# Graph kernel: tile 1's sources load first, and tile 0's counts are made after tile 1's attention

## The chip, the core and the metric

The kernel runs on one core of a Trainium2 chip. The metric is the device time of one execution in microseconds (us); three runs of the kernel before are given, and one further execution was profiled. The engines are PE (TensorE), DVE (VectorE), ACT (ScalarE), POOL (GpSimd) and SP (SyncE, which here only issues DMAs).

## The reference

A graph has 6,250 nodes with 128 features and 200,000 edges sorted by destination. An attention layer runs over the edges, then a layer norm, then two relational layers, then a layer norm:

```python
e = leaky_relu((h[src] @ Ws.T + h[dst] @ Wd.T + emb_rel[etype] @ Wr.T) @ attn_fc2_w.T, 0.01)
alpha = segment_softmax(e, dst)
agg = segment_sum(alpha[:, None] * h[src], dst)      # h itself where a node has no edge
x = layernorm(x + agg + h @ loop_weight)
for W_r, W_sl, W_el in two relational layers:
    self_msg = where(no_edge[:, None], h @ W_el, h @ W_sl)
    msg = (rel_embed[etype] + h[src]) @ W_r
    h = rrelu(segment_sum(msg, dst) * deg_isqrt + self_msg)
x = layernorm(x + h)
```

## The kernel before

**Tiles.** The nodes are cut into 50 tiles (`NT`) of 125 destinations. The edges of a tile lie in a window of 4,224 list entries, held as 128 partitions by 33 columns. A first stage loops over the tiles t = 0 to 49: it computes the attention and the first layer norm of tile t, and builds `counts[t]`, which says how many edges run from each source node to each destination of the tile. A second stage, the two relational layers, is one long row of matmuls with these counts, read back from memory, and starts when the first stage is done.

**One tile of the first stage.** SP loads the tile's lists: sources (`srcw`), destinations (`dstw`), types (`etw`), the node rows (`xt`), and in `load_wide` the destinations and types once more, broadcast to all partitions (two DMAs of 1,056 KB). POOL gathers the 4,224 source rows with 33 indirect DMAs into `rows[q]`, q = t % 2 (L559); it may start when the tile's lists are there and when PE has read what tile t - 2 left in that half (`acc_c`). DVE compares the lists with the tile's node numbers (`prepare_wide` and `prepare_edges`, one-hot masks); PE turns them into the edge terms of the attention (`terms`); ACT copies these out, SP writes them to memory and reads them back in another shape (`reshape_terms`), and DVE adds them up (DVE's `terms`). `weights` is the softmax over the edges: DVE computes `u`, and `z` at its end, with two exchanges with PE between. ACT then scales the 33 masks by exp(z), and PE multiplies them with the gathered rows (L875). DVE finishes the tile with `finalize` and `normalise`.

**Counts.** `records` packs the edge lists on DVE into 32-edge records, which SP stores. POOL gathers them (L552, 10 indirect DMAs) once for all tiles, DVE unpacks them (`recc`), PE turns them (L890) and ACT copies them to `idx`. From `idx` DVE makes one-hots in seven batches a tile, PE multiplies them (L805) and ACT copies the products into `AT`. SP's `store_counts(t)` writes `AT` to memory, 1,562.5 KB.

**What sets the order.** Each engine runs its instructions in the order in which its function is written and waits on semaphores. PE, ACT and DVE share two PSUM slots in turn, by the table `SEQ`. SP is one such order too:

```python
for t in range(NT):
    if t + 2 < NT:
        f2 = load_lists(t + 2)
        load_wide(t + 2, f2)
    ...
    if t + 1 < NT:
        reshape_terms(t + 1)
    ...
    if t < NT - 1:
        store_x1(t)
    store_counts(t)
```

So the lists of tile t + 2 are issued behind `store_counts(t - 1)`, which waits for ACT's last copy of tile t - 1's counts.

## Time and profile before

| what | value |
|---|---|
| median of 3 runs (lowest, highest) | 2778.87 us (2776.01 to 2779.62) |
| the profiled execution: its time, its span | 2776.1 us, 2774.0 us |
| mean granted TensorE clock | 0.906 |
| busy: PE, DVE, POOL, ACT | 2149.1, 2045.1, 1591.4, 1223.8 us |

Times in the rows are counted from the start of the span; the execution's own time is 2.1 us more than its span. The busy times say little alone, since the two stages have different limits: POOL works only in the first one, and PE's long row of matmuls fills the second.

### The profile page before, as it was taken

The numbers are of one execution on the slowest core, as the hardware profiler recorded it, in microseconds if no ns is written. First come the engines' busy times: TensorE is split into PE (matmuls) and PEld (weight loads), VectorE is DVE, ScalarE is ACT, GpSimd is POOL, SyncE is SP. The second block draws the span as 40 slices with busy tenths as digits, with TensorE's granted clock in tenths as the row PEclk, the third lists the DMA queues.
The fourth block names the chain that finished last, engine by engine and source line by source line (L and its number), as shares of the span: only waits on it lengthen the run. The fifth ranks groups of instructions, "written<-read, shape, count | busy, mean of one in ns | idle before, by whom it ended". The sixth has DMA issues, their size and how long they took to land.

```text
span 2774.0 us, 45483 instructions
## 1 busy us (share of the span) xinstructions
PE 2149.1 (77%) x16208; PEld 1802.6 (65%) x16208; DVE 2045.1 (74%) x4582; ACT 1223.8 (44%) x3215; POOL 1591.4 (57%) x1672
## 2 busy tenths in 40 slices
PE   1366676667767777777787788788787999999998
PEld 0255565556666666666676676676675876888887
DVE  5889998887888888888888888888797456333333
ACT  1255665555556456555555555555555323000000
POOL 6767777777777777777777777777774000000000
PEclk9988887888888988888889888999899999999999
DMA  8545554554555554554555555555454354666664
GB/s 219 145 126 173 173 153 153 157 165 152 160 175 151 156 181 146 159 183 148 160 186 151 160 190 153 168 183 156 148 177 152 112 156 133 215 211 211 217 211 158
DMA packets 184632, 463.50 MB, mean 167 GB/s; under 512 B 86336, under 2 KB 113784, under 8 KB 164577
## 3 DMA queue, kind: packets, MB, share of 16 engines
q1 hardware_dynamic: 116050, 339.10, 36.4%
q0 software_dynamic: 53600, 114.17, 16.4%
q10 hardware_dynamic: 14752, 7.26, 1.0%
q8 instruction: 132, 2.16, 0.3%
q14 instruction: 98, 0.80, 0.1%
HBM read 362.54 MB, written 97.84 MB: 166 GB/s over the span
## 4 chain that ended last, share of the span: by engine, by line
POOL 50%; PE 25%; issue 17%; DVE 6%; DMA 1%; ACT 1%; SPq 1%; ACTq 0%; POOLq 0%; DVEq 0%
POOL arena L559 50%; PE pair L951 19%; DVE arena L1114 2%; PE bank L875 1%; PE pair L924 1%; PE bank L836 1%; PE pair L954 1%; DMA wlp<-n_L_gnn_loop_weight_dram 1%; DVE arena L1084 1%; PE pair L805 1%; PE pair L782 0%; DMA group_starts<-endv 0%; SPq L434 0%; DVE arena L1194 0%; DVE arena L1092 0%
## 5 line engine op out<-in xcount | busy, mean ns | idle before, releaser
L559 POOL DMA_INDIRECT arena<-rows,srcw x1617 | 1541.6, 953 | 518.8 <-issue 491.4
L1114 DVE TENSOR_TENSOR arena<-bank,idx 128x2000 bf16<-128x2000 bf16 (+3 forms) x700 | 560.4, 853 | 21.1 <-PE pair L805 17.9
L951 PE MATMUL pair<-arena 125*125 125x384 bf16 x3285 | 551.4, 326 | 1.6 <-DVE arena L1316 1.6
L805 PE MATMUL pair<-arena 128*128 128x250 bf16 x2500 | 348.9, 287 | 260.0 <-DVE arena L1114 206.5
L581 ACT ACTIVATE arena<-pair 99x264 f32<-99x264 f32 (+2 forms) x410 | 279.0, 712 | 593.8 <-PE pair L805 448.5
L951 PEld LDWEIGHTS pair<-arena 125*125 125x125 bf16 x3285 | 447.4, 136 | 103.3 <-issue 8.4
L675 ACT ACTIVATE arena<-arena,wexp 128x128 f32<-128x128 bf16 x1650 | 487.4, 387 | 1.6
L875 PE MATMUL bank<-arena 128*125 128x130 f32 x3300 | 485.2, 318 | 0.0
L875 PEld LDWEIGHTS bank<-arena 128*125 128x125 f32 x3300 | 474.6, 230 | 4.2
L805 PEld LDWEIGHTS pair<-arena 128*128 128x128 bf16 x2500 | 239.7, 102 | 339.4 <-DVE arena L1114 267.0
L1084 DVE TENSOR_TENSOR arena<-arena,bank 128x4224 bf16<-128x4224 int16 x150 | 344.2, 2350 | 1.7
L1314 DVE SCALAR_TENSOR_TENSOR arena<-pair,norm,arena 125x128 f32<-125x128 f32 x99 | 34.6, 350 | 315.3 <-PE pair L954 270.9
L836 PE MATMUL bank<-arena 125*125 125x384 bf16 x1275 | 217.8, 328 | 2.1 <-DVE arena L1203 2.1
L782 PE MATMUL pair<-arena 128*125 128x200 bf16 x1650 | 191.4, 287 | 19.6 <-DVE arena L1114 19.6
L782 PEld LDWEIGHTS pair<-arena 128*125 128x125 bf16 x1650 | 189.5, 167 | 22.2 <-issue 20.3
L836 PEld LDWEIGHTS bank<-arena 125*125 125x125 bf16 x1275 | 170.1, 136 | 44.6 <-issue 13.9
L722 ACT ACTIVATE rstd<-mv,epst 125x1 f32<-125x1 f32 x50 | 14.7, 294 | 406.5 <-DVEq L1356 406.5
L1114 DVE TENSOR_TENSOR arena<-bank,et 128x6600 bf16<-128x6600 bf16 x50 | 179.2, 3584 | 0.0
L616 ACT ACTIVATE arena<-pair 128x500 bf16<-128x500 f32 x150 | 95.8, 638 | 72.7 <-PE pair L805 72.0
L1146 DVE TENSOR_TENSOR u<-arena,dr 128x33 f32<-128x33 f32 x50 | 10.8, 216 | 151.7 <-DMA arena<-rows,srcw 151.4
L1114 DVE TENSOR_TENSOR arena<-bank,dl 128x4224 bf16<-128x4224 bf16 x50 | 117.9, 2357 | 1.7
L795 PE MATMUL bank<-onesb,arena 128*125 128x1 bf16 x50 | 11.5, 230 | 131.2 <-issue 128.6
(250 smaller groups left out, 2312.6 us busy)
## 6 DMA issues: line engine op xcount, KB each, us to landing
arena<-counts SPq DMA_DIRECT2D x106, 812.5 KB, 4.4
counts<-arena SPq DMA_DIRECT2D x50, 1562.5 KB
arena<-dst SPq DMA_DIRECT2D x50, 1056.0 KB
arena<-etype SPq DMA_DIRECT2D x50, 1056.0 KB
arena<-rows,srcw POOLq DMA_INDIRECT x1617
arena<-counts SPq DMA_DIRECT2D x14, 281.2 KB, 2.8
edge_terms<-arena SPq DMA_DIRECT2D x200, 12.4 KB
xt<-in_x_dram SPq DMA_DIRECT2D x50, 62.5 KB
```

Source lines behind the costliest of these rows:

```text
L559: pool.indirect_dma_start(out=rows[:, q, c, :], out_offset=None, in_=rows0, in_offset=bass.IndirectOffsetOnAxis(ap=srcw[:, q, c:c + 1], ax ...
L581: act.activation(o, i, ACT.Copy).then_inc(s("ev"), 1)
L616: act.activation(AT[:, :, d0:d0 + 2 * G], two, ACT.Copy)
L675: r = act.activation(hot[:, c, :], hotb[:, c, :], ACT.Copy, scale=wexp[:, c:c + 1])
L782: r = pe.matmul(b_[0:TN, 0:R], hotb[:, c, 0:TN], toh[:, c, :], start=(c == 0), stop=(c == C - 1))
L805: r = pe.matmul(group_of(n, gi), ohl[:, sl, gi * GC + c, :], ohm[:, sl, gi * GC + c, :], start=(c == 0), stop=(c == GC - 1))
L836: pe.matmul(o, AT[0:TN, h, :], hs0[0:TN, h, :], start=(h == 0), stop=False)
L875: r = pe.matmul(sums[0:TN, 0:D + 2], hot[:, c, 0:TN], rows[:, q, c, 0:D + 2], start=(c == 0), stop=(c == C - 1))
L951: r = pe.matmul(o, ring[0:TN, m % RD, h - h0, :], hs[k][0:TN, h, :], start=(h == first), stop=(h == last - 1))
L1084: return v.tensor_tensor(out_.rearrange("p (j t) -> p j t", t=2), list_.rearrange("p (j t) -> p j t", t=2), two[:, None, :].broadcast_to(s ...
L1114: return v.tensor_tensor(hot_.rearrange("p c (j t) -> p c j t", t=2), iotap[:, 0:w].rearrange("p (j t) -> p j t", t=2)[:, None, :, :].broa ...
L1314: link(v.scalar_tensor_tensor(o, b_[0:TN, 0:D], n_, acc[0:TN, t, :], ALU.mult, ALU.add))
```

## The change

Seven things move, and nothing is computed otherwise.

1. The sources of a tile get a semaphore of their own (`ld_s0`, `ld_s1`), and POOL waits for them alone instead of for all three lists.
2. At the start of the fast path SP issues the sources of tile 1 first, then the broadcast lists of tile 0, then the short lists and node rows of tiles 0 and 1. Before, it was the padding record, the short lists of tile 0, its broadcast lists, and the lists of tile 1.
3. On POOL the wait for the lists of tile 2 stands behind the gather of the records.
4. On DVE `first_scores` comes first of all.
5. On DVE `records` comes behind the one-hots of tile 0.
6. On DVE, PE and ACT the turning of the records and the seven count batches of tile 0 go from loop turn 0 to turn 1, behind the attention weights of tile 1; `SEQ` is changed to match.
7. `normalise(0)` and the first layer's node step of tile 0 stand in front of them.

```diff
@@ order of the PSUM slots (SEQ)
     if t_ == 0:
         SEQ["types", 1] = len(SEQ)
         SEQ["turned", 1] = len(SEQ)
+        continue
+    if t_ == 1:
         for b_ in range(NGB):
             SEQ["idx", b_] = len(SEQ)
+        for j_ in range(BT):
+            SEQ["cnt", 0, j_] = len(SEQ)
     for j_ in range(BT):
         SEQ["cnt", t_, j_] = len(SEQ)
...
@@ sp_fast
-            def load_lists(t):
-                first = sp.value_load(plan_i[0:1, t:t + 1], min_val=0, max_val=E - WIN)
+            def load_sources(t, first):
+                sp.dma_start(srcw[:, t % 2, :], src[bass.ds(first, WIN)].rearrange("(p c) -> p c", c=C)).then_inc(s("ld_s%d" % (t % 2)), 16)
+
+            def window(t):
+                return sp.value_load(plan_i[0:1, t:t + 1], min_val=0, max_val=E - WIN)
+
+            def load_lists(t, first):
                 if t >= 2:
                     sp.wait_ge(s("u_done"), t - 1)
-                for a, w in ((src, srcw), (dst, dstw), (etype, etw)):
-                    if t >= 1 or a is not src:
-                        sp.dma_start(w[:, t % 2, :], a[bass.ds(first, WIN)].rearrange("(p c) -> p c", c=C)).then_inc(s("ld_w%d" % (t % 2)), 16)
+                if t >= 2:
+                    load_sources(t, first)
+                for a, w in ((dst, dstw), (etype, etw)):
+                    sp.dma_start(w[:, t % 2, :], a[bass.ds(first, WIN)].rearrange("(p c) -> p c", c=C)).then_inc(s("ld_w%d" % (t % 2)), 16)
...
+            f1 = window(1)
+            load_sources(1, f1)
+            f0 = window(0)
+            sp.wait_ge(s("st_l16"), 64)
+            load_wide(0, f0)
+            load_lists(0, f0)
+            load_lists(1, f1)
             sp.wait_ge(s("pad_ready"), 1)
             sp.dma_start(rec[E // GRAN:E // GRAN + 6], agg2[0:6, 0, 0:2 * GRAN]).then_inc(s("st_rec"), 16)
-            f0 = load_lists(0)
-            sp.wait_ge(s("st_l16"), 64)
-            load_wide(0, f0)
-            f1 = load_lists(1)
             load_wide(1, f1)
             reshape_terms(0)
...
@@ pool_fast
             for t in range(1, NT):
                 q = t % 2
-                pool.wait_ge(s("ld_w%d" % q), 48 * (t // 2 + 1) - (0 if q else 16))
                 if t == 2:
...
+                pool.wait_ge(s("ld_s%d" % q), 16 * (t // 2 + q))
                 if t >= 2:
                     pool.wait_ge(s("acc_c"), NAC * (t - 1))
...
@@ pe_fast (act_fast moves its copies in the same way)
-                if 1 <= t < NT - 1:
-                    row(t - 1)
-                if t == 0:
-                    types_in(1)
-                    types(1)
+                if t == 1:
                     for b in range(NGB):
                         n = seq("idx", b)
...
                     for j in range(BT):
                         batch(0, j)
+                if 1 <= t < NT - 1:
+                    row(t - 1)
+                if t == 0:
+                    types_in(1)
+                    types(1)
                     x1_in(0)
                     x1_node(0)
...
@@ dve_fast
+            first_scores()
             for k in range(2):
                 v.wait_ge(s("relW_ps"), k + 1)
...
-            records()
             v.wait_ge(s("st_rows"), ROWS_STORED)
             prepare_wide(0)
-            first_scores()
             prepare_edges(0)
+            records()
             terms(0)
...
                 if t == 0:
                     finalize(0)
                     prepare_edges(1)
+                    normalise(0)
+                if t == 1:
                     for b in range(NGB):
                         v.wait_ge(s("ld_rec%d" % b), 16)
...
                     for j in range(BT):
                         batch(0, j)
-                    normalise(0)
-                elif more:
+                if t >= 1 and more:
                     for j in range(2):
                         batch(t, j)
```

SP at the start of the fast path, before (`arena<-dst` and `arena<-etype` are the two broadcast lists, `edge_records<-agg` the padding record):

```order
L495 DMA edge_records<-agg 6x64 [waits pad_ready]
L441 TENSOR_LOAD plan_i
L441 ISA x2
L446 REGISTER_ALU
L446 DMA dstw<-in_dst_dram 128x33
L446 DMA etw<-in_edge_type_dram 128x33
L447 DMA xt<-in_x_dram 125x128
L454 REGISTER_ALU [waits st_l16]
L454 DMA arena<-dst 128x4224
L454 DMA arena<-etype 128x4224
```

and in the changed kernel:

```order
L448 TENSOR_LOAD plan_i
L448 ISA x2
L445 REGISTER_ALU
L445 DMA srcw<-in_src_dram 128x33
L448 TENSOR_LOAD plan_i
L448 ISA x2
L463 REGISTER_ALU [waits st_l16]
L463 DMA arena<-dst 128x4224
L463 DMA arena<-etype 128x4224
L456 REGISTER_ALU
L456 DMA dstw<-in_dst_dram 128x33
L456 DMA etw<-in_edge_type_dram 128x33
```

The sources of tile 1 go from the seventh DMA to the first, and tile 0's node rows (`xt`) from in front of the two broadcast lists to behind them.

SP in loop turn 0 of the changed kernel, from the read-back of tile 1's edge terms on (`dense_input` is `store_x1(0)`, `counts` is `store_counts(0)`, and the last two rows are the first lists of turn 1, those of tile 3):

```order
L473 DMA drw<-edge_terms 128x3x33 [waits dr_summed,dr_stored]
L485 DMA dense_input<-arena 125x128 [waits x1_ready]
L479 DMA counts<-arena 128x6250 [waits wm,ev]
L481 DMA counts<-arena 128x250 [waits ev]
L445 REGISTER_ALU [waits u_done]
L445 DMA srcw<-in_src_dram 128x33
L456 DMA dstw<-in_dst_dram 128x33
```

This piece reads as before: the sources of tile 3 still come behind the store of tile 0's counts, and that store still waits for ACT's copies (`ev`), which now belong to turn 1.

DVE at the end of turn 0 and the start of turn 1, before (the last count batches of tile 0, `normalise(0)`, the edge terms and `u` of tile 1):

```order
L1114 TENSOR_TENSOR arena<-bank,idx 128x1500 [waits pb]
L1114 TENSOR_TENSOR arena<-bank,idx 128x768
L1185 RECIPROCAL norm<-nv 125x1 [waits rs1]
L1186 RECIPROCAL nv<-nv 125x1
L1187 TENSOR_SCALAR arena<-arena,mv,nv 125x128 [waits dve_seq]
L1136 TENSOR_TENSOR dr<-drw 128x33 [waits ld_dr]
L1137 TENSOR_TENSOR dr<-dr,drw 128x33 [waits dve_seq]
L1146 TENSOR_TENSOR u<-arena,dr 128x33 [waits gath1,dr_summed]
```

and in the changed kernel, behind the one-hots of tile 1:

```order
L1148 TENSOR_SCALAR LS<-dstB 128x33
L1201 RECIPROCAL norm<-nv 125x1 [waits rs1,dve_seq]
L1202 RECIPROCAL nv<-nv 125x1
L1203 TENSOR_SCALAR arena<-arena,mv,nv 125x128 [waits dve_seq]
L1152 TENSOR_TENSOR dr<-drw 128x33 [waits ld_dr]
L1153 TENSOR_TENSOR dr<-dr,drw 128x33 [waits dve_seq]
L1162 TENSOR_TENSOR u<-arena,dr 128x33 [waits gath1,dr_summed]
```

`u` of tile 1 now follows the one-hots of its tile directly, with nothing of the counts in between.

## Rows read from the trace of the kernel before

**Rows 1.** The page, part 4: the chain that ended last, by line.

```profile
POOL arena L559 50%; PE pair L951 19%; DVE arena L1114 2%; PE bank L875 1%; PE pair L924 1%; PE bank L836 1%; PE pair L954 1%; DMA wlp<-n_L_gnn_loop_weight_dram 1%; DVE arena L1084 1%; PE pair L805 1%; PE pair L782 0%; DMA group_starts<-endv 0%; SPq L434 0%; DVE arena L1194 0%; DVE arena L1092 0%
```

**Rows 2.** Timeline of POOL: start us, us, instruction [idle before, releaser].

```profile
50.60 0.94 POOL L539 DMA_INDIRECT arena<-in_x_dram,srcw  x1 [0.30 <-issue]
...
67.43 0.95 POOL L559 DMA_INDIRECT arena<-rows,srcw  x1 [15.89 <-DMA etw<-in_edge_type_dram]
...
183.65 0.94 POOL L559 DMA_INDIRECT arena<-rows,srcw  x1 [10.82 <-PE bank L875]
```

**Rows 3.** Who waited for whom, whole run: us in total, times, longest us.

```profile
POOL arena L559 <- PE bank L875: 11.4, 3, 10.8
```

**Rows 4.** Timeline of PE, four places.

```profile
59.58 0.47 PE L753 MATMUL bank<-ident,xt 125*128 125x125 f32 x1 [13.33 <-DMA xt<-in_x_dram]
...
144.85 1.39 PE L890 MATMUL pair<-ident,arena 128*128 128x128 f32 x8
...
182.82 0.30 PE L772 MATMUL pair<-arena,Zd 125*3 125x264 bf16 x4
...
220.81 0.30 PE L772 MATMUL pair<-arena,Zd 125*3 125x264 bf16 x4
```

**Rows 5.** Timeline of DVE, from the first relation product to tile 2's preparation.

```profile
62.10 0.29 DVE L1063 CAST relW<-pair 128x128 bf16<-128x128 f32 x1 [18.46 <-PE pair L847]
...
93.43 3.48 DVE L1091 TENSOR_TENSOR arena<-arena 128x3200 f32<-128x3200 f32 x1
...
102.98 0.28 DVE L1121 TENSOR_SCALAR dl<-dstw,thr 128x66 bf16<-128x66 int32 x1
...
110.27 0.21 DVE L1146 TENSOR_TENSOR u<-arena,dr 128x33 f32<-128x33 f32 x1
...
115.51 0.41 DVE L1154 TENSOR_TENSOR_SCAN XY<-full,bank 1x128 f32<-1x128 f32 x1 [4.42 <-PE bank L862]
...
118.55 0.28 DVE L1099 TENSOR_TENSOR arena<-xt,bank 125x128 f32<-125x128 f32 x1
...
130.72 0.16 DVE L1170 TENSOR_SCALAR iso<-bank 125x1 f32<-125x1 f32 x1 [3.02 <-PE bank L875]
...
152.55 0.42 DVE L1227 COPY idx<-arena 128x100 bf16<-128x100 bf16 x2 [1.38 <-ACT arena L581]
...
171.70 0.29 DVE L1099 TENSOR_TENSOR arena<-xt,bank 125x128 f32<-125x128 f32 x1
```

**Rows 6.** Timeline of SP's DMA issues: start us, us, destination<-source.

```profile
59.87 0.52 SPq L446 DMA_DIRECT2D etw<-in_edge_type_dram  x1
...
132.81 0.34 SPq L454 DMA_DIRECT2D arena<-dst  x1
...
143.56 0.39 SPq L464 DMA_DIRECT2D drw<-edge_terms  x1
...
173.14 0.34 SPq L470 DMA_DIRECT2D counts<-arena  x1
...
175.47 0.34 SPq L446 DMA_DIRECT2D srcw<-in_src_dram  x1
```

**Rows 7.** Windows: us; length; PE, PEld, DVE, ACT, POOL busy; PEclk, DMA share, GB/s.

```profile
50.00:58.00 8.00, 0.00 (x0) 0.00 (x0) 0.00 (x0) 0.00 (x0) 1.24 (x2) 1.00 0.77 244
58.00:66.00 8.00, 2.97 (x11) 2.29 (x11) 3.49 (x13) 0.28 (x1) 0.00 (x0) 1.00 0.82 291
...
174.00:179.00 5.00, 5.00 (x32) 5.00 (x32) 5.00 (x3) 5.00 (x18) 0.00 (x0) 0.66 0.89 339
179.00:182.00 3.00, 3.00 (x30) 3.00 (x29) 2.97 (x4) 2.82 (x10) 0.00 (x0) 1.00 0.09 26
```

**Rows 8.** The DMA view: issues, count, KB each, median us to landing.

```profile
srcw<-in_src_dram SPq DMA_DIRECT2D x50, 16.5 KB, 2.1
...
arena<-in_x_dram,srcw POOLq DMA_INDIRECT x33, 9.4
```

**Rows 9.** Timeline of ACT: the last copy of tile 0's counts.

```profile
165.94 0.44 ACT L617 ACTIVATE arena<-pair 128x250 bf16<-128x250 f32 x1
```

More of the change, by code:

```diff
@@ L439, in sp_fast @@
         def sp_fast(sp):
-            def load_lists(t):
-                first = sp.value_load(plan_i[0:1, t:t + 1], min_val=0, max_val=E - WIN)
+            def load_sources(t, first):
[3 more added lines that the diff above has]
+            def load_lists(t, first):
                 if t >= 2:
                     sp.wait_ge(s("u_done"), t - 1)
-                for a, w in ((src, srcw), (dst, dstw), (etype, etw)):
-                    if t >= 1 or a is not src:
-                        sp.dma_start(w[:, t % 2, :], a[bass.ds(first, WIN)].rearrange("(p c) -> p c", c=C)).then_inc(s("ld_w%d" % (t % 2)), 16)
+                if t >= 2:
+                    load_sources(t, first)
+                for a, w in ((dst, dstw), (etype, etw)):
+                    sp.dma_start(w[:, t % 2, :], a[bass.ds(first, WIN)].rearrange("(p c) -> p c", c=C)).then_inc(s("ld_w%d" % (t % 2)), 16)
                 sp.dma_start(xt[0:TN, t % 3, :], x[t * TN:(t + 1) * TN]).then_inc(s("ld_xt%d" % (t % 3)), 16)
-                return first
             def load_wide(t, first):
@@ L506, in sp_fast @@
                 if t + 2 < NT:
-                    f2 = load_lists(t + 2)
+                    f2 = window(t + 2)
+                    load_lists(t + 2, f2)
                     load_wide(t + 2, f2)
@@ L686, in act_fast @@
                     types(1)
-                    for b in range(NGB):
-                        n = seq("idx", b)
-                        act_evac(act, n, idx[:, b * GB:(b + 1) * GB, :], slot(n)[:, :].rearrange("p (m g) -> p g m", g=GB))
-                    for j in range(BT):
-                        batch(0, j)
                     node_t(0)
@@ L694, in act_fast @@
                 elif t < NT - 1:
+                    if t == 1:
+                        for b in range(NGB):
+                            n = seq("idx", b)
+                            act_evac(act, n, idx[:, b * GB:(b + 1) * GB, :], slot(n)[:, :].rearrange("p (m g) -> p g m", g=GB))
+                        for j in range(BT):
+                            batch(0, j)
                     for j in range(3):
@@ L1057, in dve_fast, with first_scores @@
         def dve_fast(v, link):
+            def first_scores():
+                v.wait_ge(s("gath_x"), 16 * C)
+                for c0, c1 in ((0, XP), (XP, C)):
+                    w = c1 - c0
+                    link(v.tensor_tensor(prod[:, 0:w, :], rows[:, 0, c0:c1, 0:D], vb[:, None, 0:D].broadcast_to([P, w, D]), ALU.mult))
+                    link(v.tensor_reduce(rows[:, 0, c0:c1, D], prod[:, 0:w, :], AX, ALU.add))
+            first_scores()
             for k in range(2):
@@ L1085, in matches @@
                                        two[:, None, :].broadcast_to(shape), ALU.is_equal)
-            def first_scores():
-                v.wait_ge(s("gath_x"), 16 * C)
-                for c0, c1 in ((0, XP), (XP, C)):
-                    w = c1 - c0
-                    link(v.tensor_tensor(prod[:, 0:w, :], rows[:, 0, c0:c1, 0:D], vb[:, None, 0:D].broadcast_to([P, w, D]), ALU.mult))
-                    link(v.tensor_reduce(rows[:, 0, c0:c1, D], prod[:, 0:w, :], AX, ALU.add))
             def prepare_wide(t):
@@ L1119, in prepare_edges @@
                 q = t % 2
-                v.wait_ge(s("ld_w%d" % q), 48 * (t // 2 + 1) - (0 if q else 16))
+                v.wait_ge(s("ld_w%d" % q), 32 * (t // 2 + 1))
                 v.tensor_scalar(dl2[:], dstw[:, q, :][:, :, None].broadcast_to([P, C, 2]), thr[:, t:t + 1], None, ALU.subtract)
@@ L1277, in dve_fast @@
                     prepare_edges(1)
+                    normalise(0)
+                if t == 1:
                     for b in range(NGB):
@@ L1302, in dve_fast @@
                         batch(t, j)
-                else:
+                if not more:
                     finalize(t)
```

## The prediction

> **What bounds the kernel now.** I read the chain that ended last first: half of it is POOL's gathers of source rows at L559 [rows 1]. The reader should see there that the first stage is paced by the issue of gathers and not by arithmetic; PE's L951, the second stage, is the next part and is not touched. Then POOL's timeline: one gather takes 0.94 us with 0.30 us before it [rows 2], so a tile of 33 takes 33 x 1.25 = 41.3 us. Then who POOL waited for: PE's L875 three times, 11.4 us in all, 10.8 of it once [rows 3], and that once is at 183.65 us, ahead of tile 3's gathers [rows 2]. So from 183.65 us on POOL runs all but without a pause to the end of the stage. **The time of the kernel follows the start of tile 3's gathers**, unless a later tile's gathers come to wait. Work ahead of 183.65 us that doesn't move this start costs and brings nothing.
>
> Before, that start waited for `acc_c` of tile 1: PE was through with tile 1 at 182.82 us [rows 4]. The lists of tile 3 were not the limit: their sources were issued at 175.47 us [rows 6] and the transfers were over by 179 us [rows 7]. After, both have to be worked out again, and also the end of tile 2's gathers.
>
> **The start.** Sources of tile 1 first: POOL's wait at 67.43 us was for the last short list [rows 2], which SP issued at 59.87 us [rows 6], behind the broadcast lists. With the sources first it goes away, and tile 1's gathers start when the rows are stored, near 58 us, some 9 us sooner. This gain is off the path, since tile 1's rows are used much later in either kernel.
>
> `first_scores` takes 102.98 - 93.43 = 9.55 us [rows 5] and moves into the idle time ahead of 62.10 us, where DVE waited 18.46 us. It needs all gathers of x: the last is issued at 50.60 us [rows 2] and lands in 9.4 us by the median [rows 8], so it runs from 60.0 to 69.6 us. But `xt` of tile 0 now queues behind the broadcast lists. Before it landed in front of them, and PE's L753 ran at 59.58 us [rows 4]. The DMA engines were busy with the row stores up to 58 us, and the window 58 to 66 us moved 291 GB/s x 8 us = 2.3 MB [rows 7], about the two broadcast lists (2.1 MB); the list behind them landed at 67.43. Issued sooner they still wait for the row stores, so I let them fill the same window and `xt` land at 67.2 us. The first relation product reached DVE 62.10 - 59.58 = 2.5 us behind L753, so DVE takes it up at 69.7 instead of 62.10 us: of the 9.55 us won, 7.6 are given back.
>
> From there to `u` of tile 0 DVE had no wait: 110.27 - 62.10 = 48.2 us [rows 5], less 9.55 for the scores that are gone, so `u` comes at 69.7 + 38.6 = 108.3 us. The wait of 4.42 us behind it was for PE, which was in the middle of `types_in(0)`. With `records` now between the one-hots and `u`, PE has long done that; I leave 1.2 us of it for the exchange itself (an estimate; 0 and 4.4 are its ends). `z` of tile 0 then stands at 108.3 + (118.55 - 110.27) - 3.2 = 113.4 us, 5.2 us sooner than the 118.55 of before.
>
> **Tile 1.** ACT's scaling and PE's L875 took 130.72 - 118.55 = 12.2 us: over at 125.6 us. SP issued the next broadcast lists 2.1 us later (132.81), and the read-back of the edge terms 10.75 us behind that (143.56) [rows 6]: 127.7 and 138.4 us. This round trip was hidden under the turning of the records and tile 0's counts. Now DVE, with 8.8 us of `finalize` and one-hots and 0.6 of `normalise` (my estimates from the same timeline), is free at 135 us, so about 5 us of it stand open: a new wait at DVE's `terms(1)`. A small list on an empty queue lands in 2.1 us [rows 8]; 140.5, and `u` of tile 1 at 141.0 us. `weights` took 118.55 - 110.27 - 3.2 = 5.1 us; with the node step inside it I take 5.5: `z` at 146.5 us. From there to the end of L875 it was 182.82 - 171.70 = 11.1 us [rows 4, 5]: **acc of tile 1 is done at 157.6 us instead of 182.82**. That is what the change brings where POOL waited.
>
> **Tile 2's gathers** need the records stored: they are ready at 107.9 us (`u` of tile 0 less its edge terms). With 7 us for the store they land at 115, and 43 gathers x 1.25 us end at 169 us. So by these two terms POOL could go on at 169 us, 14.7 us sooner.
>
> **What is late next.** SP. The sources of tile 3 are issued behind `store_counts(0)`, and that waits for ACT's last copy of tile 0's counts. Before, the copy ended at 165.94 + 0.44 = 166.4 us [rows 9], and the store went at 173.14 us. Now it is made in turn 1. PE's edge terms of tile 2 end 2.1 us behind acc: 159.7 us. The turning of the records, as PE and ACT share it, took 152.55 - 144.85 = 7.7 us: 167.4 us. The seven batches with the last copy took 166.4 - 152.55 = 13.8 us: **181.2 us**. Queued behind this wait on SP are all lists of tile 3, its broadcast lists and the edge terms of tile 2. The store goes out at 181.3 us, the sources 175.47 - 173.14 = 2.3 us later, at 183.6 us. Before, the traffic of store and lists lasted from 173.14 to about 179 us (339 GB/s up to 179, 26 behind it [rows 7]), so I take the sources to land 5.9 us behind the store: 187.2 us, and POOL starts at 187.5 us.
>
> What the row shows here is a small list that lands only when the large transfer ahead of it is through: the list issued at 59.87 us was waited for until 67.43 us [rows 2, 6], where an empty queue takes 2.1 us. The Trainium skill (DMA: Bandwidth & Descriptors, section "Queues, rings and completion order") says that an SDMA engine consumes descriptors in ring order, but that a later one may finish its write before an earlier one, and that completion is not FIFO. If the sources so came in 2.1 us behind their issue, POOL would start at 186 us, which is +2.4 us instead of +3.9. The sum goes by the row.
>
> **Sum.** 187.5 - 183.65 = +3.9 us. Behind it tile 3's gathers end at 228.8 us. Acc of tile 2 ended at 220.81 us before; DVE begins tile 1's own batches about 1.5 us sooner than it did, so acc comes near 219.3 us and tile 4's gathers don't wait. The profiled execution would be 2776.1 + 3.9 = 2780.0 us; it lies 2.8 us under the median of the runs shown, so the median goes to 2778.87 + 3.9 = 2782.8 us, +0.14%. A change under 0.2% (5.6 us) can't be told from none here.
>
> **Rivals.**
> - *The sources of tile 3 don't queue behind the store*: +2.4 us, 2781.3 us. For it: the list is small. Against it: the row above. 0.12.
> - *Slower*: tile 1's edge terms come late. The records' gathers (10 of 128 x 512 words, 2.6 MB) run from 115 to 127.5 us, and the broadcast lists of tile 2 go out at 127.7 us. At 291 GB/s the gathers alone are 9 us of traffic. If the record store lands over 2 us later than I take it, both share the DMA engines, and each us at the read-back is a us at the store of counts. Half of the 9 us gives +4.5 on top: +8.4 us, 2787.3 us. It decides from 1.7 us more on. For it: every step up to 181.2 us is a chain without slack, and no step of it was so tight before. Against it: the broadcast lists met the tail of these gathers before too. 0.30.
> - *Faster*: the chain is shorter than I take it, so that the sources are in by 183 us or the store doesn't hold them. Then POOL starts when tile 2's gathers end, but DVE is the bound behind it: tile 4's gathers wait for acc of tile 2 at 219.3 instead of starting at 183.65 + 41.3 = 224.9 us, so at most -5.6 us, 2773.3 us. It needs over 4 us less in the chain. 0.10.
> - The forecast itself, with ends of its own from -1 (no exchange wait, `xt` 3 us sooner) to +8 us (all of the 4.42 us left, PE at its lower clock in the turning): 2778 to 2787. 0.48, of which 0.05 lie over the bound.
>
> **How the numbers follow.** Faster: a little over half of the third rival, 0.06. Slower: 0.30 + 0.05 = 0.35. The same: 0.59. The range takes in the forecast's own ends and most of the slower rival: 2776 to 2790 us.
>
> **What would show it.** In POOL's timeline tile 1 starts near 58 to 60 us, the records' gathers near 115, and tile 3's first gather idles from about 169 to 187 us, with the sources of tile 3 as its releaser and not PE's L875 counterpart. DVE has a wait of some 5 us for the read-back ahead of `u` of tile 1, near 141 us. ACT's last copy of tile 0's counts is at 181 us and SP's store of counts just behind it. It is wrong if POOL's long pause is gone or short, if the last copy comes before 178 us or after 185, or if POOL pauses again at tile 4 or later.

## The result and the profile after

| | changed kernel | kernel before, same set of runs |
|---|---|---|
| median (lowest to highest), 22 runs each | 2781.27 us (2777.59 to 2785.55) | 2778.29 us (2775.41 to 2780.66) |
| ratio, 95% interval | 1.0013 [1.0007, 1.0019] | |
| the profiled execution: time, span | 2784.27 us, 2782.2 us | 2776.1 us, 2774.0 us |
| mean granted TensorE clock | 0.901 | 0.906 |

The changed kernel is 3.0 us slower by the medians, 0.13%, with an interval of 1.9 to 5.3 us. That is inside the bound of 0.2% for "the same". The interval leaves out 1, so the loss is small but real.

The page of the changed kernel, part 4, the chain by line, has POOL's gathers first as in [rows 1]:

```profile
POOL arena L572 52%; PE pair L966 19%; PE bank L889 1%; DVE arena L1130 1%; PE bank L850 1%; PE pair L939 1%; DMA wlp<-n_L_gnn_loop_weight_dram 1%; PE pair L969 1%; DMA group_starts<-endv 0%; DMA arena<-in_x_dram,srcw 0%; PE pair L819 0%; DVE arena L1107 0%; PE pair L796 0%; DVE arena L1077 0%; DVE arena L1078 0%
```

Who POOL waited for, whole run (us in total, times, longest us):

```profile
POOL arena L572 <- DMA srcw<-in_src_dram: 25.0, 2, 17.0
...
POOL arena L564 <- DMA edge_records<-arena: 3.2, 1, 3.2
```

PE is gone from this list: the 10.8 us of [rows 3] have become 17.0 us behind a load. POOL's timeline says where:

```profile
60.05 3.87 POOL L572 DMA_INDIRECT arena<-rows,srcw  x1 [7.99 <-DMA srcw<-in_src_dram]
...
115.14 0.95 POOL L564 DMA_INDIRECT arena<-edge_records,gidx  x1 [3.21 <-DMA edge_records<-arena]
...
185.83 0.95 POOL L572 DMA_INDIRECT arena<-rows,srcw  x1 [17.00 <-DMA srcw<-in_src_dram]
...
227.16 0.95 POOL L572 DMA_INDIRECT arena<-rows,srcw  x1 [0.30 <-issue]
```

Tile 1 starts at 60.05 us instead of 67.43, the gathers of the records start at 115.14, and tile 2's last gather ends at 185.83 - 17.00 = 168.8 us. Then POOL stands still until 185.83 us, 2.2 us later than the 183.65 of [rows 2]. Tile 4 follows at 227.16 us without a pause, and POOL pauses nowhere after it.

DVE's timeline, from the first scores to the first count batch:

```profile
59.60 3.49 DVE L1077 TENSOR_TENSOR arena<-arena 128x3200 f32<-128x3200 f32 x1 [16.16 <-DMA arena<-in_x_dram,srcw]
...
69.16 0.29 DVE L1086 CAST relW<-pair 128x128 bf16<-128x128 f32 x1
...
107.73 0.21 DVE L1162 TENSOR_TENSOR u<-arena,dr 128x33 f32<-128x33 f32 x1
...
109.57 0.41 DVE L1170 TENSOR_TENSOR_SCAN XY<-full,bank 1x128 f32<-1x128 f32 x1 [1.02 <-PE bank L876]
...
113.02 0.28 DVE L1115 TENSOR_TENSOR arena<-xt,bank 125x128 f32<-125x128 f32 x1
...
124.17 0.16 DVE L1186 TENSOR_SCALAR iso<-bank 125x1 f32<-125x1 f32 x1 [2.00 <-PE bank L889]
...
139.90 0.20 DVE L1152 TENSOR_TENSOR dr<-drw 128x33 f32<-128x33 f32 x1 [6.24 <-DMA drw<-edge_terms]
...
140.42 0.21 DVE L1162 TENSOR_TENSOR u<-arena,dr 128x33 f32<-128x33 f32 x1
...
144.98 0.28 DVE L1115 TENSOR_TENSOR arena<-xt,bank 125x128 f32<-125x128 f32 x1
...
166.37 0.42 DVE L1243 COPY idx<-arena 128x100 bf16<-128x100 bf16 x2 [1.41 <-ACT arena L594]
```

The reader should see two waits: 4.42 us at the exchange of tile 0 [rows 5] is 1.02 us now, and a new one of 6.24 us stands ahead of `dr` of tile 1, for the read-back of the edge terms. `u` of tile 1 still comes at 140.42 us, 25 us sooner than in the kernel before, where DVE had the batches of tile 0 ahead of it:

```profile
165.38 0.21 DVE L1146 TENSOR_TENSOR u<-arena,dr 128x33 f32<-128x33 f32 x1
```

PE's timeline: the node rows of tile 0 (L767), the product of tile 1 (L889) and the first of tile 2's edge terms behind it (L786), then the same place a tile later:

```profile
64.86 0.47 PE L767 MATMUL bank<-ident,xt 125*128 125x125 f32 x1 [19.02 <-DMA xt<-in_x_dram]
...
146.65 10.10 PE L889 MATMUL bank<-arena 128*125 128x130 f32 x66
156.69 0.30 PE L786 MATMUL pair<-arena,Zd 125*3 125x264 bf16 x4
...
218.57 0.30 PE L786 MATMUL pair<-arena,Zd 125*3 125x264 bf16 x4
```

So PE had read tile 1's rows at 156.7 us, 26.1 us sooner than the 182.82 of [rows 4], and nobody waited for it. ACT's last copy of tile 0's counts and what SP issued around it:

```profile
179.43 0.45 ACT L630 ACTIVATE arena<-pair 128x250 bf16<-128x250 f32 x1
```

```profile
126.26 0.35 SPq L463 DMA_DIRECT2D arena<-dst  x1
...
137.88 0.39 SPq L473 DMA_DIRECT2D drw<-edge_terms  x1
...
179.90 0.34 SPq L479 DMA_DIRECT2D counts<-arena  x1
...
182.27 0.35 SPq L445 DMA_DIRECT2D srcw<-in_src_dram  x1
```

Copy to 179.88 us, store at 179.90, sources at 182.27, gather at 185.83: from 168.8 us on POOL had nothing to wait for but this list, and all of that is lost in SP's row behind one store. Windows over the store and the list (columns as in [rows 7]) show the traffic in between:

```profile
182.00:184.00 2.00, 0.95 (x8) 0.61 (x8) 1.97 (x4) 0.00 (x0) 0.00 (x0) 1.00 0.95 400
184.00:186.00 2.00, 0.00 (x0) 0.00 (x0) 2.00 (x2) 0.57 (x1) 0.17 (x1) 1.00 0.68 177
```

### The profile page after: what moved, and what is told of

Its sections match the earlier page's. It is cut to its first block, busy times and chain, and to the rows that moved or that the text cites. A ratio compares the mean times of both kernels' runs of the same rounds, so it can differ in the third digit from the quotient of the medians.

```text
span 2782.2 us, 45483 instructions
## 1 busy us (share of the span) xinstructions
PE 2156.0 (77%) x16208; PEld 1808.7 (65%) x16208; DVE 2044.6 (73%) x4582; ACT 1223.6 (44%) x3215; POOL 1595.9 (57%) x1672
## 4 chain that ended last, share of the span: by engine, by line
POOL 52%; PE 24%; issue 18%; DVE 4%; DMA 2%; ACT 0%; SPq 0%; POOLq 0%; ACTq 0%; DVEq 0%
POOL arena L572 52%; PE pair L966 19%; PE bank L889 1%; DVE arena L1130 1%; PE bank L850 1%; PE pair L939 1%; DMA wlp<-n_L_gnn_loop_weight_dram 1%; PE pair L969 1%; DMA group_starts<-endv 0%; DMA arena<-in_x_dram,srcw 0%; PE pair L819 0%; DVE arena L1107 0%; PE pair L796 0%; DVE arena L1077 0%; DVE arena L1078 0%
## 5 line engine op out<-in xcount | busy, mean ns | idle before, releaser
L889 PE MATMUL bank<-arena 128*125 128x130 f32 x3300 | 489.9, 321 | 0.0
L889 PEld LDWEIGHTS bank<-arena 128*125 128x125 f32 x3300 | 479.9, 232 | 3.5
L796 PEld LDWEIGHTS pair<-arena 128*125 128x125 bf16 x1650 | 187.6, 166 | 12.4 <-issue 10.8
```

The costliest lines, as they stand in the source:

```text
L796: r = pe.matmul(b_[0:TN, 0:R], hotb[:, c, 0:TN], toh[:, c, :], start=(c == 0), stop=(c == C - 1))
L889: r = pe.matmul(sums[0:TN, 0:D + 2], hot[:, c, 0:TN], rows[:, q, c, 0:D + 2], start=(c == 0), stop=(c == C - 1))
```

## The experiments

Twelve runs were made in four sets. In two sets every execution took about 4,550 us, that of the kernel before too. They say little about a change of 3 us and stand at the end of this section. One of the two other sets ran on the same chip as those two, so the chip alone is not the reason. The kernels of these two other sets are compared with executions of the kernel before of their own set, whose medians were 2777.98 us and, for the sources of tile 3 alone, 2777.20 us.

**Only the loads and DVE's start.** The changed kernel, with the turning and the count batches of tile 0 back in turn 0 on DVE, PE and ACT. PE's part of it (ACT's is alike, `SEQ` follows, and on DVE `normalise(0)` goes back behind the batches; the first loop is the turning):

```diff
                 if t == 0:
                     types_in(1)
                     types(1)
+                    for b in range(NGB):
+                        n = seq("idx", b)
...
+                    for j in range(BT):
+                        batch(0, j)
                     x1_in(0)
                     x1_node(0)
-                if t == 1:
-                    for b in range(NGB):
-                        n = seq("idx", b)
...
-                    for j in range(BT):
-                        batch(0, j)
```

> The kernel of e2 again: the changed kernel with the turning of the records and the counts of tile 0 in turn 0, as before. My theory: u of tile 1 near 159.3, acc of tile 1 near 176.8, tile 3's gathers start near 177.2 us instead of 183.65: 6.4 us under the kernel before, ratio 0.9977. Rival (the loads part gives back what it gains): within 2 us of the kernel before.

Measured: 2772.75 us, ratio 0.9982 [0.9973, 0.9991], 5.2 us less than before. `u` of tile 1 is at 159.15 us, and POOL:

```profile
177.43 0.94 POOL L568 DMA_INDIRECT arena<-rows,srcw  x1 [8.34 <-PE bank L884]
```

PE is the releaser, as before, 6.2 us sooner (183.65 [rows 2]). The sources were issued at 169.25 us and did not matter. So this half of the change is a gain by itself.

**Only the counts.** The kernel before, with the turning and the batches of tile 0 moved to turn 1 and `normalise(0)` ahead of them, and nothing else of the change:

```diff
                 if t == 0:
                     types_in(1)
                     types(1)
-                    for b in range(NGB):
-                        n = seq("idx", b)
...
-                    for j in range(BT):
-                        batch(0, j)
                     x1_in(0)
                     x1_node(0)
+                if t == 1:
+                    for b in range(NGB):
+                        n = seq("idx", b)
...
+                    for j in range(BT):
+                        batch(0, j)
```

> The kernel of e3 again: the kernel before with the turning of the records and the counts of tile 0 in turn 1, nothing else. My theory: the last copy of tile 0's counts near 184.5 us, tile 3's gathers start near 190.4 us instead of 183.65: 6.7 us over the kernel before, ratio 1.0024. Rival (acc of tile 1 is what tile 3's gathers wait for in every order): they start near 173 and the time is up to 5 us under the kernel before.

Measured: 2786.19 us, ratio 1.0029 [1.0019, 1.0040], 8.2 us more than before. POOL:

```profile
192.09 0.94 POOL L563 DMA_INDIRECT arena<-rows,srcw  x1 [19.21 <-DMA etw<-in_edge_type_dram]
```

The last copy ends at 185.72 us, the store goes at 185.75, the sources at 188.13, and POOL, which in this kernel waits for all three lists, starts 8.4 us later than before. The two halves, -5.2 and +8.2 us, add up to the +3.0 us of the whole. The starts of tile 3 do too: -6.2 + 8.4 = +2.2. The start is 1.7 us later than the 190.4 expected: the last copy came 1.2 us later than the 184.5, and the rest lies between it and POOL's start.

**All lists of tile 3 ahead of the store.**

```diff
-                if t + 2 < NT:
+                if t == 1:
+                    load_wide(3, f3)
+                elif t + 2 < NT:
...
                     store_x1(t)
+                if t == 0:
+                    f3 = window(3)
+                    load_lists(3, f3)
                 store_counts(t)
```

The broadcast lists of tile 3 stay in their place.

> The kernel of e1 again, since on the first chip every execution, that of the kernel before too, took some 1,770 us more and the engines stood still for reasons that the trace doesn't name. The changed kernel, with SP issuing the lists and node rows of tile 3 ahead of store_counts(0). My theory (the store holds the sources of tile 3): tile 3's gathers start near 169 us instead of 185.8, tile 4's at acc of tile 2, near 218.6 instead of 227.2; 5 to 6 us under the kernel before, ratio 0.998. Rival (the lists don't matter, DVE is late): the same as the changed kernel, 3 us over the kernel before. Second rival (the time follows tile 3's start alone): 14 us under it.

Measured: 2773.86 us, ratio 0.9985 [0.9976, 0.9994]. SP issued the sources at 142.25 us, tile 3's gathers followed tile 2's at 170.12 us without a pause, and the wait came one tile later, for PE's product of tile 2, as the third rival of the prediction had it:

```profile
221.59 0.95 POOL L577 DMA_INDIRECT arena<-rows,srcw  x1 [10.38 <-PE bank L894]
```

Tile 4 starts 5.6 us before the 227.16 of the changed kernel, not the 8.6 expected: `u` of tile 1 was 1.5 us later in this execution, and the last copy 2.2 us later (182.11). The edit isn't the reason for all of this: DVE's first relation product, long before the two kernels differ, was already 1.1 us later (70.28 against 69.16).

**The sources of tile 3 alone ahead of the store.**

```diff
                 if t >= 2 and t != 3:
                     load_sources(t, first)
...
                     store_x1(t)
+                if t == 0:
+                    f3 = window(3)
+                    sp.wait_ge(s("u_done"), 2)
+                    load_sources(3, f3)
                 store_counts(t)
```

> The changed kernel, but SP issues the sources of tile 3 alone ahead of the store of tile 0's counts; the other lists of tile 3 stay behind it. Theory (POOL's 17.0 us were the sources' place in SP's row alone): tile 3's first gather follows tile 2's last near 169 us, the last copy of tile 0's counts stays within 1 us of 179.9 us, and tile 4's gathers wait for PE's product of tile 2 at 218.6 us instead of starting at 227.2: 8 us less than the changed kernel, a ratio to before of 0.998, and about 3 us less in tile 4's start than with all lists moved (221.6). Rival (POOL's work beside the batches slows DVE, since both are then busy from 169 to 183 us): the last copy moves past 181 us and tile 4's gathers to 221 us or later.

Measured: 2772.22 us, ratio 0.9984 [0.9975, 0.9993]: 8.1 us under the changed kernel by the two ratios. ACT's last copy, and POOL at tile 4:

```profile
180.35 0.45 ACT L634 ACTIVATE arena<-pair 128x250 bf16<-128x250 f32 x1
```

```profile
219.66 0.94 POOL L576 DMA_INDIRECT arena<-rows,srcw  x1 [9.16 <-PE bank L893]
```

One DMA of 16.5 KB moved in front of one store gives the 8 us. The last copy ends at 180.80 us, 0.9 us later than in the changed kernel, and 0.6 of that was there before POOL's earlier gathers began (DVE's first `idx` copy at 166.95 us against 166.37). That leaves 0.3 us for POOL's gathers beside the batches, and the rival falls. The two medians of this kernel and the one with all lists moved, 1.6 us apart in different sets, don't tell them apart. Their traces have tile 4 1.9 us apart, but 0.9 of that stands at the first relation product already (69.38 against 70.28), where both kernels are alike. In the five executions that share the code up to there this product comes between 68.76 and 70.28 us, so single traces don't resolve 1 us. That the broadcast lists make a difference is not shown either: in both kernels they stand behind the store.

**And the turning back in turn 0, behind the node step.** The lists of tile 3 ahead of the store as above; the turning of the records goes back to turn 0 (where DVE had the new wait of 6.24 us), and only the batches stay in turn 1:

```diff
                     x1_in(0)
                     x1_node(0)
+                    for b in range(NGB):
+                        n = seq("idx", b)
...
                 if t == 1:
-                    for b in range(NGB):
-                        n = seq("idx", b)
...
                     for j in range(BT):
                         batch(0, j)
```

> The kernel of e1 with the turning of the records (not the counts) in turn 0 again, behind the node step of tile 0, where DVE waits 6.2 us for the edge terms. My theory: DVE is through with the turning near 147 us, u of tile 1 near 147.5 us (140.4 in the changed kernel), acc of tile 1 near 163, the last count batch of tile 0 near 174.5 (177.9), acc of tile 2 near 215 us (218.6). Tile 3's gathers start near 169, tile 4's near 215: some 10 us under the kernel before, ratio 0.9965, and 3 to 4 us under e1b. Rival (the wait for the edge terms was slack that nothing can fill, since the records come late): the same as e1b within 1 us.

Measured: 2768.05 us, ratio 0.9967 [0.9955, 0.9979], the best of all. `u` of tile 1 is at 146.66 us, later than in the changed kernel, but DVE takes up the batches at 160.72 us, 6.1 us before the 166.37 + 0.45 of the changed kernel, and the last copy ends at 175.63 us instead of 179.88. Not all of the 6.1 us arrive there, since PE takes up the batches only at 165.25 us, behind tile 1's product and tile 2's edge terms, and that is 3.4 us sooner than in the changed kernel (168.68). DVE's timeline there, then POOL's at tile 4:

```profile
155.74 4.61 DVE L1112 TENSOR_TENSOR arena<-arena,bank 128x4224 bf16<-128x4224 int16 x2
160.27 0.42 DVE L1248 COPY idx<-arena 128x100 bf16<-128x100 bf16 x2
160.72 1.80 DVE L1135 TENSOR_TENSOR arena<-bank,idx 128x2000 bf16<-128x2000 bf16 x2
```

```profile
214.89 0.94 POOL L577 DMA_INDIRECT arena<-rows,srcw  x1 [5.20 <-PE bank L894]
```

**The runs at 4,550 us.** The first set held four kernels whose edits are those above. The changed kernel again:

> The changed kernel unaltered, timed and profiled once more, to see how far two executions of one kernel differ. My theory (the time follows the start of tile 3's gathers, 185.8 us here against 183.65 before): that start comes again within 1 us of 185.8, and the time is 2 to 5 us over the kernel before; the mean distance between the starts of two tiles' gathers, 41.38 us in the changed kernel's trace and 41.30 in that of before, is chance and may come out anywhere from 41.28 to 41.42. Rival (the change makes POOL's gathers themselves slower): the distance is again 41.36 or more.

Measured: 4550.18 us, ratio 0.9985 [0.9972, 0.9998]. All lists of tile 3 ahead:

> The changed kernel with one thing moved: SP issues the three lists and node rows of tile 3 ahead of store_counts(0) instead of behind it. My theory (the store of tile 0's counts holds the sources of tile 3): tile 3's gathers start when tile 2's end, near 169 us instead of 185.8; tile 4's then wait for acc of tile 2, which stays near 218.6 us, and start there instead of at 227.2: 8.4 us less than the changed kernel, 2772.9 us, which is 5 to 6 us less than the kernel before. Rival (the turning and the counts in turn 1 make DVE late, and the lists don't matter): no change against the changed kernel, 2781 us. Second rival (the time follows tile 3's start alone): 17 us less, 2764 us.

Measured: 4553.57 us, 0.9992 [0.9980, 1.0004]. Only the loads and DVE's start:

> The changed kernel with one part undone: the turning of the records and the counts of tile 0 stand in turn 0 again, as before; the order of the loads, POOL's own semaphore, first_scores first and records later are kept. My theory: u of tile 1 comes near 159.3 us (165.4 before), acc of tile 1 ends near 176.8 us (182.8 before), the sources of tile 3 are in by 173, so tile 3's gathers start near 177.2 us instead of 183.65 and the time is 6.4 us under the kernel before, 2771.9 us. Rival (the loads part gains nothing, since xt behind the broadcast lists gives it back and the move of the counts cost nothing either): within 2 us of the kernel before, 2778 us.

Measured: 4546.80 us, 0.9984 [0.9966, 1.0002]. Only the counts:

> The kernel before with one part of the change alone: the turning of the records and the counts of tile 0 go to turn 1, nothing else. My theory: the read-back of tile 1's edge terms at 143.6 us now stands open, u of tile 1 near 146, z near 150.5, acc near 161.6 us; the last copy of tile 0's counts near 184.5 us, the sources of tile 3 in near 190, tile 3's gathers start near 190.4 us instead of 183.65: 6.7 us over the kernel before, 2785.0 us. With e2 the two parts then add up to about what the change shows. Rival (acc of tile 1 is what tile 3's gathers wait for in every order): they start at 173, tile 2's end, and the time is up to 5 us under the kernel before.

Measured: 4557.27 us, 1.0010 [1.0000, 1.0020].

The second set held the changed kernel once more, the sources of tile 3 alone ahead, and the sources on ACT's queue (below). The changed kernel:

> The changed kernel once more, on the chip of the next two runs. It has two uses. If the 8.2 us that its profiled span was longer than that of before, against 3.0 us between the medians, are scatter between executions, this profile gives a span between 2776 and 2784 us, while tile 3's first gather stands at 185.8 us again, within 0.3, with the sources of tile 3 as its releaser. If the changed order makes every later gather slower (rival), the gathers of the tiles from 3 to 49 take 41.38 us a tile again and the span is near 2782. The median is expected at 2781 us, a ratio of 1.001.

Measured: 4539.21 us, 0.9973 [0.9957, 0.9990]; its tile 3 starts at 231.18 us, so its question, whether the start repeats and whether the changed order makes later gathers slower, can't be answered here; the text below the table in the next section answers it. The sources of tile 3 alone ahead:

> The changed kernel, but SP issues the sources of tile 3 alone ahead of the store of tile 0's counts; the other lists of tile 3 stay behind it. Theory (POOL's 17.0 us were the sources' place in SP's row alone): tile 3's first gather follows tile 2's last near 169 us, the turning and the batches keep their times (last copy 179.9 us), and tile 4's gathers wait for PE's product of tile 2 at 218.6 us instead of starting at 227.2: 8.3 us less than the changed kernel in the profile, ratio to before 0.998. This is also 3 us better than with all lists of tile 3 moved, since there the broadcast lists ran beside the records' gathers. Rival (POOL's work beside the batches slows DVE, since both are then busy from 169 to 183 us): the last copy moves to 182 us or later and tile 4's gathers to 221 us or later, no better than with all lists moved, 2773.9 us.

Measured: 4545.60 us, 1.0001 [0.9986, 1.0016]. Here who waited for whom of the changed kernel (second set) reads:

```profile
ACT arena L594 <- remote: 1855.6, 111, 42.2
POOL arena L572 <- PE bank L889: 1653.0, 47, 39.9
DVE arena L1130 <- remote: 1432.8, 55, 39.0
```

POOL waited for PE at 47 tiles, and ACT and DVE, which PE needs, for something that the profile names only as "remote". What it is stays open. With POOL waiting at every tile, the start of tile 3 decides nothing, and these ratios are no verdict on the change. The first 250 us can still be read for the one question that the last kernel was for.

**The sources of tile 3 from ACT's queue.** The changed kernel, but:

```diff
@@ sp_fast, load_lists
-                if t >= 2:
+                if t >= 2 and t != 3:
                     load_sources(t, first)
@@ act_fast, turn 1
                         for j in range(BT):
                             batch(0, j)
+                        act.wait_ge(s("u_done"), 2)
+                        act.dma_start(srcw[:, 1, :], src[bass.ds(f3, WIN)].rearrange("(p c) -> p c", c=C)).then_inc(s("ld_s1"), 16)
```

> The changed kernel, but the sources of tile 3 are issued from ACT's queue right behind its last copy of tile 0's counts, beside the store of the counts and not behind it in SP's queue. Theory (a small list behind the store in one queue is held until the store's bytes are through): the list is issued near 180.3 us and lands 2.1 to 3 us later, so tile 3's first gather is at 182.5 to 183.5 us and the time 2 to 3 us under the changed kernel, ratio to before near 1.000. Rival (the DMA engines are full whatever the queue): the list lands with the store's bytes, tile 3's first gather stays near 185.8 us, ratio 1.001.

Measured: 4532.20 us, ratio 0.9961 [0.9946, 0.9977]. The timeline of ACT, SP and POOL in that kernel:

```profile
251.00 0.36 ACTq L711 DMA_DIRECT2D srcw<-in_src_dram  x1
251.37 0.45 ACT L630 ACTIVATE arena<-pair 128x250 bf16<-128x250 f32 x1
251.85 0.34 SPq L479 DMA_DIRECT2D counts<-arena  x1
...
252.83 0.95 POOL L572 DMA_INDIRECT arena<-rows,srcw  x1 [49.29 <-DMA srcw<-in_src_dram]
```

and in the changed kernel of the same set:

```profile
224.83 0.45 ACT L630 ACTIVATE arena<-pair 128x250 bf16<-128x250 f32 x1
225.30 0.34 SPq L479 DMA_DIRECT2D counts<-arena  x1
...
227.68 0.35 SPq L445 DMA_DIRECT2D srcw<-in_src_dram  x1
...
231.18 0.95 POOL L572 DMA_INDIRECT arena<-rows,srcw  x1 [53.62 <-DMA srcw<-in_src_dram]
```

The DMA view gives some landings here, in us behind the issue. The sources in the ACT kernel, then the store and the sources in the changed kernel:

```profile
srcw<-in_src_dram ACTq DMA_DIRECT2D x1, 16.5 KB, 1.6
...
counts<-arena SPq DMA_DIRECT2D x1, 1562.5 KB, 5.2
...
srcw<-in_src_dram SPq DMA_DIRECT2D x1, 16.5 KB, 3.2
```

So in the changed kernel the store lands at 225.30 + 5.2 = 230.5 us and the list at 227.68 + 3.2 = 230.9, behind it.

From the start of ACT's last copy to the gather it is 1.46 us against 6.35 us (and 6.40 us in the changed kernel at 2784 us, so this piece is the same there). Of the 4.9 us, 1.7 are the landing (1.83 us from issue to gather against 3.50), the rest is the earlier issue: 0.37 us ahead of the copy's start instead of 2.85 behind it. It is more than the 2.3 to 3.3 us expected, because the list went 0.37 us ahead of the copy's start and not right behind its end. The rival isn't decided: the list was issued 0.85 us ahead of the store, so it never ran beside the store's bytes in another queue. What is shown is that landing behind the store costs the list 1.7 us, and being issued behind it about 3.

## Why the prediction came out right

Its forecast was +3.9 us; the medians say +3.0, and the start of tile 3's gathers, on which the sum was made, says +2.2. The path and the waits were those of the forecast. The closeness of the number is in part luck: the median of 2781.27 us is the 2781.3 us of the first rival (a list that doesn't queue behind the store), though the traces show that the list did queue. The start came out lower than forecast because the chain was shorter, and not by the rival's reason.

- **What bounds the kernel** held in every kernel, with tile 4 in place of tile 3 where tile 4 had to wait:

| kernel | tile 3 starts | tile 4 starts | median | median less tile 4 |
|---|---|---|---|---|
| before | 183.65 | 224.95 | 2778.29 | 2553.3 |
| changed | 185.83 | 227.16 | 2781.27 | 2554.1 |
| loads alone | 177.43 | 218.73 | 2772.75 | 2554.0 |
| counts alone | 192.09 | 233.40 | 2786.19 | 2552.8 |
| all lists ahead | 170.12 | 221.59 | 2773.86 | 2552.3 |
| sources ahead | 169.51 | 219.66 | 2772.22 | 2552.6 |
| turning back | 168.65 | 214.89 | 2768.05 | 2553.2 |

The medians come from three sets, in which the kernel before had medians of 2777.2 to 2778.3 us. The median is tile 4's start plus 2553.2 us, within 1.0 us, over starts that lie 18.5 us apart. The profiled executions scatter more: span less tile 4's start is 2550.5, 2551.3, 2551.0, 2551.8 and 2551.7 us in the five experiments (in the table's order), 2549.1 in before and 2555.0 in the changed kernel. So of the 8.2 us between the two profiled spans 2.2 are the start, and 6.0 are these two executions. Of the 6.0, 3.8 lie in POOL's gathers: from tile 4's first to tile 49's last it is 1902.4 us in the changed kernel and 1898.6 in before. The three kernels that hold the whole change and move only lists or the turning besides have 1898.3, 1898.8 and 1898.3 us, so the changed order doesn't make later gathers slower.

- **The start.** Tile 1's first gather near 58 us: 60.05, and by the profile its last releaser was the list of sources, issued at 51.12 us behind the row stores, and not the stores. `first_scores` 60.0 to 69.6 us: 59.60 to 69.12. `xt` was taken to land at 67.2 us and to hold the relation products until 69.7: it was there at 64.86, and DVE took the products up at 69.16, held by the scores. The two ends lay close together, so the 2.3 us by which `xt` was misjudged moved this start by 0.5.
- **Tile 0.** `u` 108.3 us predicted, 107.73 measured. The exchange wait taken as 1.2 us was 1.02; z 113.4 against 113.02. Scaling and product took 11.15 us instead of 12.2, acc came at 124.17 instead of 125.6: PE's granted clock was 0.81 in the mean from 114 to 124 us (half until about 117, full from 119), where before it was 0.72 from 120 to 131 (half until 125, full from 127), and L889 took 9.47 us where L875 had taken 10.49. This is scatter and not the change: in the five experiments the same product took 9.46 to 10.37 us, and the 9.46 is also that of the kernel with the counts alone, whose code up to there is that of before.
- **Tile 1.** The round trip of the edge terms took 11.62 us (126.26 to 137.88) instead of 10.75 and landed 2.02 us later: the new wait was 6.24 us instead of about 5, `u` 140.42 instead of 141.0. z came 4.56 us behind it (5.5 taken), acc at 156.69 instead of 157.6.
- **Tile 2's gathers.** 115 and 169 us predicted; 115.14 and 168.8 measured.
- **What is late next.** This is the step that carried the sign. One thing about the store is missing from the working: `store_counts(0)` also waits for the first weights of tile 1 (`wm`). In the kernel before, that wait ended last, since the copy was done at 166.4 us and the store went at 173.14. The change brought these weights forward and the copies back, and so the copy is the last wait now. Turning done at 167.4 predicted, 166.37 measured; last copy 181.2 against 179.88; store 181.3 against 179.90; sources 183.6 against 182.27; start 187.5 against 185.83. Of the 1.7 us by which POOL started sooner than forecast, 1.3 are the chain up to the last copy, and 0.35 lie between the copy and POOL's start.
- **The landing.** The list was taken to land 5.9 us behind the store. POOL started 5.93 us behind it, at 185.83, as the traffic of 400 GB/s ran out in the windows above. By the rival, 2.1 us behind the issue, it would have been 184.4. So the row was right to be followed. The 2.1 us is no median of the 50 loads, as the working reads it: the DMA view has a landing for one of them only, in the first 30 us. In the changed kernel at 4,539 us the landings are on record, and the list lands 0.4 us behind the store. Issued from ACT's queue ahead of the store, the same list let POOL start 1.83 us behind its issue. The Trainium skill (DMA: Bandwidth & Descriptors, "Queues, rings and completion order") says that a DMA engine takes its descriptors in ring order and that a later one may finish its write before an earlier one, but also that the increment of a semaphore lands only after every earlier write of that DMA engine. The trace agrees with the last part: at 4,550 us it is 3.50 us from the issue to the gather behind the store, against 1.83 ahead of it, and no row here shows the list overtaking. Whether the list's bytes or only its semaphore came behind the store is not told apart.
- **Slower**, the rival with 0.30: the last gather of the records was issued at 126.41 us and the broadcast lists at 126.26, and the read-back took 0.9 us more (11.62 instead of 10.75), half of the 1.7 from which it decides. The other four kernels with the new order of the loads have 11.28 to 11.69 us, the one with the counts alone 10.56. That the records' gathers are the cause fits, but isn't isolated. **Faster**, with 0.10: it needed the sources in by 183 us. The experiments show that its size was right: with the sources moved, tile 4's wait for PE ends at 219.66 us where 219.3 had been worked out for tile 2's product, and the time is 5.0 us under before, where at most 5.6 had been.

The expected gain was real, then: PE frees tile 1's rows 26 us sooner, and the half of the change that needs nothing of the counts is worth 5.2 us alone. It was turned into a new wait, because the counts' store went late and the sources of tile 3 stand behind it.

## What to carry to other kernels

When work is moved behind other work, look at the queue that stores its result: everything issued behind that store moves with it, however small, here 16.5 KB that cost 8 us. Issue a list that paces another engine ahead of any store that waits on data. And take the time of a paced kernel from the last place at which the pacing engine waited, over the medians of several kernels, not from the spans of two single executions.

## What the runs showed of the hardware

- A gather's issue on POOL takes 0.95 us, but 3.87 us at 60.05 us, when DVE had begun a product of two f32 operands in SBUF (L1077, 59.60 to 63.09) just before, while under the reduction with one operand behind it the gathers took their normal time. POOL's record ends 0.83 us after DVE's. In the kernel before, the same product ran from 93.43 to 96.91 us, and the gather at 94.30 took 3.43 us and ended 0.82 us after it. The Trainium skill (SBUF — State Buffer, "SBUF: two separate sides") says that a DVE operation with two SBUF inputs, against a GpSimd operation that reads SBUF, takes the port pair that the two share for the whole instruction if it starts first, and that the other blocks fully. The trace agrees: the gather reads its indices from SBUF, and took 3.87 instead of 0.95 us.
- ACT's queue issued a DMA at 251.00 us that stands behind the copy begun at 251.37 us in its program, and while the copy before that one ran (250.86 to 251.50): the issue didn't wait for these two copies, and no semaphore in the kernel asks for it.
